# Cross-attention: the first tile of probabilities of six batches in eight is turned by a DRAM round trip and VectorE, and mixes begin with the high halves

## The reference

```
q = (x @ w_q), k = (context @ w_k), v = (context @ w_v)      # 16 heads of 64
sim = einsum('bhid,bhjd->bhij', q, k) * SCALE
attn = softmax(sim, axis=-1)
out = einsum('bhij,bhjd->bhid', attn, v) @ w_o + b_o
```

## Time and profile before

| what | value |
|---|---|
| median of 3 runs | 1588.15 us (1588.05 to 1588.57) |
| profiled execution | 1588.07 us, its span 1586.2 us |
| TensorE busy | 99% of the span, granted clock 1.00 |
| VectorE, ScalarE, GpSimd busy | 78%, 64%, 51% |
| DMA queue q1 | 44.3% of 16 engines' span |

### The profile page before, as it was taken

How to read it: one execution, slowest core, us unless ns; L and a number is a source line. 1 busy time by engine, 2 the same in 40 slices (tenths; PEclk the granted TensorE clock), 3 DMA queues, 4 the chain that set the end, 5 groups by cost and what they waited for, 6 DMA issues and landing times. The chain is left out here.

```text
span 1586.2 us, 30382 instructions
## 1 busy us (share of the span) xinstructions
PE 1570.0 (99%) x11114; PEld 1376.8 (87%) x11114; DVE 1243.0 (78%) x2411; ACT 1020.1 (64%) x2025; POOL 816.3 (51%) x780
## 2 busy tenths in 40 slices
PE   9999999999999999999999999999999999999998
PEld 7889899898999989999899888988988887888886
DVE  6558878787888878878788685767777889989887
ACT  3457777777777777777787442445446666676765
POOL 3317657376573856747455232334334555555554
PEclk9999999999999999999999999999999999999999
DMA  8984636456364654635443684432436601010010
GB/s 253 273 256 150 179 112 186 128 168 178 116 185 120 179 164 128 184 111 151 140 111 95 188 285 138 133 93 80 137 94 228 238 14 61 20 43 31 14 48 27
DMA packets 203412, 215.60 MB, mean 136 GB/s; under 512 B 83776, under 2 KB 149632, under 8 KB 203264
## 3 DMA queue, kind: packets, MB, share of 16 engines
q1 hardware_dynamic: 203264, 213.66, 44.3%
HBM read 154.88 MB, written 58.72 MB: 135 GB/s over the span
## 5 line engine op out<-in xcount | busy, mean ns | idle before, releaser
L79 PE MATMUL p_bank_score<-p_ctxt,p_qo 128*128 128x256 f32 x2304 | 304.5, 286 | 0.7 <-ACT p_probs L1105 0.3
L79 PEld LDWEIGHTS p_bank_score<-p_ctxt,p_qo 128*128 128x128 f32 x2304 | 288.1, 191 | 5.8 <-issue 2.1
L79 PE MATMUL p_bank_mix<-p_probt,p_ctx 128*128 128x512 f32 x1152 | 292.1, 398 | 0.5
L79 PEld LDWEIGHTS p_bank_mix<-p_probt,p_ctx 128*128 128x128 f32 x1152 | 207.4, 189 | 41.9 <-issue 3.8
L1307 DVE SCALAR_TENSOR_TENSOR p_qo<-p_bank_mix,p_odd,p_qo 128x512 fp32r<-128x512 f32 x192 | 143.8, 749 | 57.7 <-ACT p_qo L1119 50.1
L1119 ACT ACTIVATE p_qo<-p_bank_mix,p_odd 128x512 fp32r<-128x512 f32 x192 | 132.3, 689 | 68.1 <-PE p_bank_mix L79 67.7
L1105 ACT ACTIVATE p_probs<-p_bank_score,p_small 128x257 f32<-128x257 f32 x256 | 121.3, 475 | 59.6 <-DVE p_small L1288 55.6
L794 POOL TENSOR_SCALAR p_probs<-p_probs,p_small 128x256 f32<-128x256 f32 x256 | 121.4, 480 | 71.3 <-DVE p_small L1294 71.2
L788 POOL TENSOR_TENSOR p_ctx<-p_ctx_in,p_ctx 128x768 fp32r<-128x768 f32 x64 | 118.3, 1848 | 68.1 <-ACT p_ctx L1094 67.7
L783 POOL TENSOR_TENSOR p_ctx_in<-p_ctx_in,p_odd_in 128x768 f32<-128x768 f32 x64 | 118.1, 1846 | 40.7 <-DMA p_odd_in<-in_ctx_dram 40.7
L1288 DVE TENSOR_REDUCE p_small<-p_bank_score 128x1 f32<-128x257 f32 x256 | 105.3, 414 | 10.7 <-PE p_bank_score L79 7.9
(11 more groups left out here) (302 smaller groups left out, 3910.7 us busy)
## 6 DMA issues: line engine op xcount, KB each, us to landing
p_blocks_in<-in_ctx_dram SPq DMA_DIRECT2D x256, 96.0 KB, 2.4
p_ctx_in<-in_ctx_dram SPq DMA_DIRECT2D x64, 384.0 KB, 3.2
q<-p_ctx SPq DMA_DIRECT2D x64, 256.0 KB, 3.6
ffn<-p_w_raw SPq DMA_DIRECT2D x64, 256.0 KB, 3.0
p_odd_in<-in_ctx_dram SPq DMA_DIRECT2D x64, 192.0 KB, 3.6
p_x<-in_x_dram SPq DMA_DIRECT2D x32, 256.0 KB, 4.2
p_quad<-q SPq DMA_DIRECT2D x32, 256.0 KB, 3.7
p_probt<-q SPq DMA_DIRECT2D x32, 256.0 KB, 3.9
```

The lines of the kernel that those rows point to most:

```text
L79: made = e.matmul(out, lhsT, rhs, start=n == 0, stop=n == last)
```

## The change

In batches 1 to 6 of each group of 8 (`is_moved`), tile 0 of the probabilities no longer goes through TensorE.

- GpSimd's `scale(b, 0)` writes its result into a free part of `probt` with the columns rearranged, after a wait for `mixed` of batch b-2.
- SyncE stores it to DRAM (`put_rows`, 128 KB, placed ahead of load_context) and reads it back as 32-row blocks (`move_blocks`, four DMAs of 32 KB with 256-byte pieces, placed between load_blocks and load_odd).
- VectorE turns the blocks (`turn_moved(b-1)`, 128x256) between turn_context(b+1,0) and low_probs(b-1,1) of the next batch.
- ScalarE makes the high half (`high_moved(b-1)`, 128x256) between exponent(b,0) and high_turned(b+1,0); GpSimd makes the low half (`low_moved(b-1)`, 128x256) between low_context(b) and scale(b,0).
- `turn_probs(b, 0)` has two transposes instead of four; high_probs and low_probs of half 0 are 256 wide instead of 512.
- Every mix now makes its four products with the high half of the probabilities first and the two with the low half last; for m = 0 it waits for the high halves before the first and for the low halves before the fifth.

```diff
+            def put_rows(b):
+                e.wait_ge(normal, b * NT + 1)
+                e.dma_start(p_dram[b % 2], moved_from(b)).then_inc(rows_put, DMA)
+            def move_blocks(b):
+                e.wait_ge(rows_put, DMA * moves(b))
+                for q in range(NQD):
+                    e.dma_start(moved_to(b)[q * QUAD:(q + 1) * QUAD, :].rearrange("r (h n) -> r h n", h=HT),
+                                p_dram[b % 2, :, q * SP * QUAD:(q + 1) * SP * QUAD].rearrange(
+                                    "(h r) n -> r h n", r=QUAD)).then_inc(blocks_moved, DMA)
...
+                    if is_moved(b):
+                        put_rows(b)
                     if b + 2 < B:
                         load_context(b + 2)
...
                             load_blocks(b + 2)
+                    if is_moved(b):
+                        move_blocks(b)
+                    if b + 2 < B:
                         load_odd(b + 2)
...
+                to, made = probs[n % 6][:, 0:KEYS], probs[n % 6][:, 0:KEYS]
+                if tile == 0 and is_moved(b):
+                    e.wait_ge(mixed, KC * (b - 1))
+                    to = moved_from(b).rearrange("p (q s k) -> p s q k", s=SP, k=QUAD)
+                    made = made.rearrange("p (s q k) -> p s q k", s=SP, k=QUAD)
+                e.tensor_scalar(to, made, small[n % 4][:, 2:3], 1.0, ALU.mult, ALU.mult).then_inc(normal, 1)
+            def low_moved(b):
+                e.wait_ge(moved_hi, moves(b))
+                e.tensor_tensor(probt[b % 2][:, LO, :, 0:P], turned_to(b), f32(probt[b % 2][:, HI, :, 0:P]),
+                                ALU.subtract).then_inc(moved_lo, 1)
...
                 low_context(b)
+                if is_moved(b - 1):
+                    low_moved(b - 1)
...
-                for i in range(2):
+                for i in (1,) if half == 0 and is_moved(b) else (0, 1):
...
-                    e.wait_ge(probt_lo, 2 * (b + 1))
+                    e.wait_ge(probt_hi, 2 * (b + 1))
+                    if is_moved(b):
+                        e.wait_ge(moved_hi, moves(b))
...
+                for h in (HI, LO):
+                    for s in range(SP):
+                        e.matmul(b_mix[m], ctx[i][:, h, s, cols], probt[i][:, HI, s, :], start=h == HI and s == 0,
+                                 stop=False)
+                if m == 0:
+                    e.wait_ge(probt_lo, 2 * (b + 1))
+                    if is_moved(b):
+                        e.wait_ge(moved_lo, moves(b))
+                for s in range(SP):
+                    made = e.matmul(b_mix[m], ctx[i][:, HI, s, cols], probt[i][:, LO, s, :], start=False,
+                                    stop=s == SP - 1)
+                made.then_inc(mixed, 1)
...
+            def high_moved(b):
+                e.wait_ge(blocks_turned, moves(b))
+                e.activation(probt[b % 2][:, HI, :, 0:P], turned_to(b), ACT.Copy).then_inc(moved_hi, 1)
...
                     exponent(b, 0)
+                    if is_moved(b - 1):
+                        high_moved(b - 1)
...
+            def turn_moved(b):
+                e.wait_ge(blocks_moved, DMA * NQD * moves(b))
+                e.transpose(turned_to(b).rearrange("p s (h r) -> p h s r", r=QUAD),
+                            moved_to(b).rearrange("p (h s k) -> p h s k", s=SP, k=QUAD)).then_inc(blocks_turned, 1)
...
+                        if is_moved(b - 1):
+                            turn_moved(b - 1)
                         if not first:
                             low_probs(b - 1, 1)
                         top(b, 1)
```

More of the change, by code:

```diff
@@ L243, in __init__, with cross_attention @@
         self.late_in = room.sem_ring("late_in", 3)
-def cross_attention(nc, kept, stack, ident, ident_ready, x_rows, w_q, w_k, w_v, w_o, b_o, ctx_dram, q_dram, o_dram,
+def cross_attention(nc, kept, stack, ident, ident_ready, x_rows, w_q, w_k, w_v, w_o, b_o, ctx_dram, q_dram, p_dram, o_dram,
                     x1_dram, moments, w_attn, w_proj, w_1, w_2, ffn_dram):
@@ L307, in cross_attention @@
             ctxt = [carve(second, f"ctxt{i}", [P, 2, KC, KEYS], F32R) for i in range(2)]
+            with ExitStack() as between:
+                carve(between, "probt0_high", [P, SP, ROW])
+                moving = [carve(between, "moving0", [P, SP, ROW])]
             probt = [carve(second, "probt0", [P, 2, SP, ROW], F32R)]
+            with ExitStack() as between:
+                carve(between, "probt1_high", [P, SP, ROW])
+                moving.append(carve(between, "moving1", [P, SP, ROW]))
             with ExitStack() as boundaries:
@@ L374, in probs_bank, with is_moved, moves, moved_from @@
             return b_probt
+        def is_moved(b):
+            return 0 < b % GB < GB - 1
+        def moves(b):
+            return b // GB * (GB - 2) + b % GB
+        def moved_from(b):
+            return moving[b % 2][:, 0, 2 * P:2 * P + KEYS]
+        def moved_to(b):
+            return probs[b * NT % 6][:, 0:KEYS]
+        def turned_to(b):
+            return moving[b % 2][:, :, 0:P]
         FIRST_TWO = [(b, 1 + 4 * b) for b in range(2)]
+        def probs_rows(b, half, side):
+            first = P if half == 0 and is_moved(b) else 0
+            return (probt[b % 2][:, side, :, half * 2 * P + first:(half + 1) * 2 * P],
+                    probs_bank(b, half).rearrange("p (s r) -> p s r", s=SP)[:, :, first:2 * P])
         def turned_in(b):
@@ L1099, in exponent @@
                     e.wait_ge(probs_turned, (n - 6) // 2 + 1)
+                if n >= 6 and (n - 6) % NT == 0 and is_moved((n - 6) // NT):
+                    e.wait_ge(blocks_turned, moves((n - 6) // NT))
                 if tile == 0 and b > 0 and b % GB == 0:
@@ L1113, in high_probs @@
                 e.wait_ge(probs_turned, 2 * b + half + 1)
-                e.activation(probt[b % 2][:, HI, :, half * 2 * P:(half + 1) * 2 * P],
-                             probs_bank(b, half).rearrange("p (s r) -> p s r", s=SP), ACT.Copy).then_inc(probt_hi, 1)
+                hi, bank = probs_rows(b, half, HI)
+                e.activation(hi, bank, ACT.Copy).then_inc(probt_hi, 1)
+            def high_moved(b):
+                e.wait_ge(blocks_turned, moves(b))
+                e.activation(probt[b % 2][:, HI, :, 0:P], turned_to(b), ACT.Copy).then_inc(moved_hi, 1)
             def high_mix(b, m):
@@ L1299, in low_probs @@
                     e.wait_ge(o_gone[0], DMA * NT // 2 * (b // GB))
-                hi, lo = (probt[b % 2][:, s, :, half * 2 * P:(half + 1) * 2 * P] for s in (HI, LO))
-                e.tensor_tensor(lo, probs_bank(b, half).rearrange("p (s r) -> p s r", s=SP), f32(hi),
-                                ALU.subtract).then_inc(probt_lo, 1)
+                (hi, bank), (lo, _) = (probs_rows(b, half, s) for s in (HI, LO))
+                e.tensor_tensor(lo, bank, f32(hi), ALU.subtract).then_inc(probt_lo, 1)
+            def turn_moved(b):
+                e.wait_ge(blocks_moved, DMA * NQD * moves(b))
+                e.transpose(turned_to(b).rearrange("p s (h r) -> p h s r", r=QUAD),
+                            moved_to(b).rearrange("p (h s k) -> p h s k", s=SP, k=QUAD)).then_inc(blocks_turned, 1)
             def low_mix(b, m):
```

10 lines of the change are left out of this document (4 added, 6 removed).

## The result

The changed kernel takes 1615.01 us (median of 4 runs, 1612.39 to 1617.00), the kernel before 1588.19 beside it: ratio 1.0167, interval 1.0155 to 1.0180. Forecast was 1593.0 in a range of 1577 to 1606. It is slower, as was held likelier than faster, by 26.8 us where 4.9 had been summed up.

What follows compares the result with a forecast made beforehand. TensorE, busy 99% of the span, was taken as the bound, at 9.33 us a batch. 1588.07 - 12.8 + 7.0 + 4.0 + 4.6 + 2 = 1592.9, and with 0.1 for the runs' median 1593.0; whole range 1577 to 1606.

Steps and rivals of the forecast that it cites:

- Removal: TensorE: two transposes dropped in each of 48 batches, 0.109 us each, 10.4 us less; moved batches need 9.11 instead of 9.33.
- Mixes with the high halves first: A group's last mix: TensorE no longer waits for VectorE's low half, 0.3 us in each of 8 groups, 2.4 us less.
- Tile 1 is wanted earlier and comes later: Batches 2 to 6 of 7 groups: inserted engine work delays tile 1's scale, TensorE stalls 0.2 us each, 7.0 us added.
- The last group: w_o's split shifts the chain there, so TensorE stalls 0.8 us in each of 5 batches: 4.0 us added (3.2 to 4.7).
- A loop on SyncE and GpSimd: Weights' load behind put_rows, which waits for scale(b,0): one turn 9.7 us against 9.31, 4.6 us added in 6 groups.
- Does the round trip itself come in time?: From one turn_moved to the next 9.2 to 9.6 us against 9.31: 0 to 9 us added, 2 taken.
- the round trip decides: Rival, chance 0.18: small pieces queue behind 640 KB, last block lands 3.0 after issue, 1615 us; at 2.5, 1601.
- The rule on pieces below 512 bytes: Skill's rule against the change: smaller pieces are read, modified, written below line rate; prediction saw no more than 0.4 here.

Runs made afterwards that it cites:

- removal: Changed kernel with batches 2 to 6 moved, but DMAs, turn_moved, high_moved, low_moved and the waits for them left out: 1580.12 us (0.9950).
- engines: Changed kernel without put_rows and move_blocks; turn_moved waits for tile 0's scale in place of the blocks: 1585.94 us (0.9987).
- wsmall: Changed kernel in full, with four of five loads of the third block's weights cut to 64 KB: 1604.56 us (1.0104).
- putonly: Changed kernel without move_blocks; put_rows stays and VectorE turns tile 1's rows, so nothing waits for blocks coming back: 1608.06 us (1.0122).
- nowait: Changed kernel with every DMA and engine instruction, but VectorE turns tile 1's rows, so only the tile's buffer waits for the round trip: 1607.25 us (1.0118).
- actput: Changed kernel with put_rows issued from ScalarE's queue, behind exponent(b,1): 1606.71 us (1.0120).
- both: Changed kernel with put_rows issued from ScalarE's queue and GpSimd's low_moved(b-1) behind scale(b,0): 1608.15 us (1.0125).
- putlate: Changed kernel with put_rows issued behind load_context and the weights' load, right before load_blocks: 1619.09 us (1.0200).
- hold: Kernel of engine work alone (no DMA added) plus SyncE's wait for tile 0's scale at put_rows' place in moved batches: 1593.72 us (1.0033).

## Why the prediction was wrong

- **Removal.** Right in mechanism: 96 transposes less, batches of 9.12 (9.11 forecast), 0.10 us each, but in the last group 9.27.
- **Mixes with the high halves first.** Wrong: 2.4 us forecast, 0.4 measured, which can't be told from none. The hole went, as said, 0.36 us in that group, and its time was given back 5 us later. I had not asked what is late next.
- **Tile 1 is wanted earlier and comes later.** Right in mechanism: TensorE waits for GpSimd's scale of tile 1 before the transposes. Forecast 0.2 a batch, measured 9.23 - 9.12 = 0.11, so 3.9 us and not 7.0. turn_moved takes 0.40 and high_moved 0.42 (0.42 and 0.39 taken).
- **The last group.** Nearly right: 9.84 a batch against 9.11 + 0.8. Of it 0.57 is stall (9.27 in `removal`), so 2.9 us and not 4.0.
- The engine part of the sum was 1588.1 - 12.8 + 7.0 + 4.0 = 1586.3 and `engines` took 1585.9. That is partly luck: the gain was some 3 us too large (9.6 measured: 1588.1 less 1578.5) and the stalls 3.6 too large (7.4 measured). The error of the forecast, 29.1 measured against 6.6, is in the two steps on transfers.
- **A loop on SyncE and GpSimd.** The loop exists (25.6 us of GpSimd's waiting, `wsmall`), and the landing of 3.8 was well taken (median 3.7, the longest 5.6: load issued at 576.27, cast at 581.83). But GpSimd's lateness itself reached tile 1's scale in only 2 of 30 late batches. What more it costs must go through SyncE's queue, where put_rows waits for tile 0's scale and load_blocks stands behind; `wsmall` gives 10 us back. The step also left out that the next load waits for the stores' landing; in the change SyncE waited for that 7 times, 3.1 us in all.
- **Does the round trip itself come in time?** This is the step that failed. Its own wait was mis-sized: 2 us taken, 7.8 measured; a block lands in 2.6 (median) and not 2.0 to 2.4. (Its items add up to 9.1 to 9.5, not 9.2 to 9.6, which doesn't change this.) What it did not have at all is the first half of its own chain read as a loop: turn_context frees the buffer, load_blocks fills it again, turn_context waits. I used load_blocks only as something that holds SyncE for 1.86 us. Before, that loop is 3.88 + 0.03 + some 1.4 for the issues in front of the last + 2.4 = 7.7, 1.6 short of a batch (an estimate from the earlier trace rows). Each item of the change took a piece: 0.40 from the insertions on VectorE, 0.6 from SyncE's order, 0.9 from the later landing, 0.2 from the batch being shorter. No single piece reaches 1.6. Where weights pass, the piece of the landing is larger still, and the loop closes only there and in the batch behind. `putonly` has VectorE's wait in full, 22 us over `engines`, with no round trip to wait for.
- The rival **the round trip decides** gave 1615 at a landing of 3.0, and 1615.0 is what was measured. That is an accident of numbers: the landing was 2.6, at 2.5 the rival says 1601, and without any wait for the round trip the kernel still takes 1607. Its argument in favour, transfers that queue behind 640 KB issued just ahead, was right, but the victim is load_blocks.
- The rule on pieces below 512 bytes (the Trainium skill, "DMA: Bandwidth & Descriptors", Specifications) is not what decided: a quarter of the bytes and pieces with as many issues gives back 5 us, and without any of the reads in small pieces the kernel is as slow (`putonly` against `nowait`). The 64 KB loads of the earlier trace rows, which the prediction set against this rule, have pieces of 512 bytes (L1712, 128 values), so they don't bear on it.
- The section on the anatomy of one DMA (the Trainium skill, "DMA: Bandwidth & Descriptors"), which the prediction cites for a fixed part, gives its 2.0 us for DMAs that GpSimd issues. Those here are SyncE's, and the sum went by the rows.

What stays open: why put_rows' wait and its DMA together cost 22 where they cost 7.8 and 0.2 apart; the landing (2.9 and 3.3) and the gap in front of it go the right way, and the trace shows that it is the wait for the blocks that costs, but which of the 14 us belong to 128 KB more and which to 0.36 us of issue wasn't tried. Nor is it fully shown why taking put_rows off SyncE (`actput`, `both`) gives back 8 only. In `both` the 9.7 us of waiting for low_moved are one part. Also, SyncE waits 42.6 us, 25 times, for the weights' stores to land before it issues the next load (45.6 in `actput`, 3.1 in the change), and load_blocks stands behind that, so the weights' loop is a candidate; `both` with small weights was not run. The Trainium skill ("DMA: Bandwidth & Descriptors", section Issuing engines are not separate DMA queues) says that DMAs of all issuing engines end up on the same 16 engines and interleave. The traces agree with it: put_rows lands in 1.7 us ahead of the loads on SyncE's queue, in 3.1 behind them on the same queue (`putlate`), and in 3.1 from ScalarE's queue (`actput`), where it meets them too.

## What to carry to other kernels

Before adding a DMA that waits to a shared queue, list what stands behind it, and for each of those find the buffer that it fills and who waits for that: that loop (free, issue, land, use) has a slack of its own, and it must be summed even if nobody waits there now. An in-order queue that is held lets its transfers go in a bunch, so count their landings as they are in a bunch, not as the medians of the trace before. And a forecast that hits the time by another mechanism is wrong; only a run that removes the wait in question tells.

## What the runs showed of the hardware

- The landing of one and the same 96 KB load grows as a 384 KB load in front of it comes closer: 2.4, 2.9 and 3.3 us at 2.64, 1.44 and 1.09 us (the last with a 128 KB store in front as well). A 256 KB load between them adds to it: in `hold` 3.3 with one, 2.7 without.
- A quarter of the bytes needn't land sooner: in `wsmall` the weights' loads of 64 KB took 3.2 us, those of 256 KB 3.3.
- The four issues of load_blocks hold SyncE for 1.8 us (median) in the kernel before, in the change and in `both`; the longest took 3.1, 2.9 and 3.3.
- A DMA of 128 KB that waits for nothing cost the kernel 0.2 us in 48 uses, its landing 3.0 us; one of the same size behind a wait landed in 1.7 and cost 22 with its wait, of which the wait alone cost 7.8.
